# Two halves of a running sum on VectorE, and four later key-rounding steps on ScalarE

## The reference

```
q_hk = (hidden_q @ Wq.T).reshape(Bv, Sv, H, K)
q_big = jnp.einsum('bshk,hkq->bshq', q_hk, w_kc_q)          # then rope
kv_r = _apply_rope(kv_c, sin_k[None], cos_k[None])
q_r = jnp.einsum('bshq,hqr->bhsr', q_big, W_qr)
k_r = jnp.einsum('bld,hdr->bhlr', kv_r, W_kr)
scores = jnp.einsum('bhsr,bhlr->bhsl', q_r, k_r)
attn = jax.nn.softmax(scores, axis=-1)                       # over 1444 keys
ctx_c = jnp.einsum('bhsl,bld->bhsd', attn, kv_r)
```

## Time and profile before

| | us |
|---|---|
| median of 3 runs (3305.87 to 3306.35) | 3306.21 |
| time of the profiled execution | 3314.55 |
| its span | 3312.8 |
| mean granted TensorE clock | 0.929 of full |
| TensorE matmuls busy | 2855.9 (86%) |
| VectorE busy | 2276.1 (69%) |
| GpSimd busy | 1749.6 (53%) |
| ScalarE busy | 1658.2 (50%) |

### The profile page before, as it was taken

How to read it: one execution, slowest core, us unless ns; L and a number is a source line. 1 busy time by engine, 2 the same in 40 slices (tenths; PEclk the granted TensorE clock), 3 DMA queues, 4 the chain that set the end, 5 groups by cost and what they waited for, 6 DMA issues and landing times. The chain is left out here.

```text
span 3312.8 us, 62826 instructions
## 1 busy us (share of the span) xinstructions
PE 2855.9 (86%) x18352; PEld 1925.8 (58%) x18352; DVE 2276.1 (69%) x4050; ACT 1658.2 (50%) x3458; POOL 1749.6 (53%) x1268
## 2 busy tenths in 40 slices
PE   5999979999799899898998999899989989996335
PEld 4777769999655565565555555556556556553123
DVE  5778764444376676677677667767767667666887
ACT  1333322222147646647646655654764664663556
POOL 0000012322167757667666666766765766763566
PEclk9888879999899999999999999999999999998566
DMA  4000010000201100000100000010110100011100
GB/s 112 0 0 0 0 48 10 5 10 10 75 6 25 22 12 21 19 16 17 23 18 17 21 18 17 16 26 7 24 22 11 22 19 16 11 50 35 42 13 25
DMA packets 130259, 71.17 MB, mean 21 GB/s; under 512 B 83582, under 2 KB 124510, under 8 KB 129880
## 3 DMA queue, kind: packets, MB, share of 16 engines
q1 hardware_dynamic: 129944, 67.45, 8.2%
HBM read 56.95 MB, written 10.04 MB: 20 GB/s over the span
## 5 line engine op out<-in xcount | busy, mean ns | idle before, releaser
L1200 POOL TENSOR_TENSOR c_psum<-c_p 120x800 f32<-120x800 f32 (+1 forms) x384 | 758.4, 1980 | 454.3 <-ACT c_p L1514 199.8
L1514 ACT ACTIVATE c_p<-c_s_ps 120x400 f32<-120x400 f32 (+1 forms) x1536 | 650.9, 513 | 301.7 <-PE c_s_ps L1686 231.3
L1698 PE MATMUL c_o_ps<-c_p,c_val 120*64 120x400 f32 (+1 forms) x3072 | 614.8, 523 | 10.9 <-ACT c_onum L1479 10.9
L1279 DVE TENSOR_REDUCE c_mpart<-c_m_ps 128x1 f32<-128x484 f32 x416 | 271.4, 652 | 204.3 <-PE c_m_ps L1593 204.2
L1324 DVE TENSOR_TENSOR c_acc<-c_acc,c_psum 120x800 f32<-120x800 f32 x256 | 370.2, 1446 | 59.9 <-POOL c_psum L1200 57.9
L1593 PE MATMUL c_m_ps<-c_kmax,c_q 64*128 64x484 f32 x1080 | 308.4, 438 | 90.6 <-DVE c_mpart L1279 49.1
L1191 POOL TENSOR_TENSOR l_rr<-c_psum,l_rr 96x400 f32<-96x400 f32 x256 | 264.2, 1053 | 190.5 <-DVE l_rr L1346 190.4
L1698 PEld LDWEIGHTS c_o_ps<-c_p,c_val 120*64 120x64 f32 (+1 forms) x3072 | 191.5, 139 | 281.1 <-issue 163.5
L1682 PE MATMUL c_s_ps<-c_q,c_k 64*120 64x400 f32 (+1 forms) x1536 | 321.4, 370 | 1.7 <-ACT c_p L1514 1.7
L1285 DVE CUSTOM_DVE_ANT_0 c_xt<-c_m_ps,c_xt,c_mpart 128x484 fp32r<-128x484 f32 x360 | 259.8, 722 | 86.5 <-DVE c_mpart L1279 45.4
L1629 PE MATMUL c_s_ps<-c_xt,l_a 128*96 128x400 f32 x1536 | 310.4, 352 | 9.8 <-DVE l_rr L1346 8.0
(11 more groups left out here) (259 smaller groups left out, 5304.6 us busy)
## 6 DMA issues: line engine op xcount, KB each, us to landing
c_rdb<-l_denominators SPq DMA_DIRECT2D x128, 100.0 KB, 2.7
c_kv<-in_ctx SPq DMA_DIRECT2D x32, 360.0 KB
c_mrow<-c_mneg SPq DMA_DIRECT2D x288, 0.5 KB, 2.0
x_rows<-in_x SPq DMA_DIRECT2D x4, 800.0 KB
x_spill<-x_rows SPq DMA_DIRECT2D x8, 400.0 KB
l_xa<-x_spill SPq DMA_DIRECT2D x8, 400.0 KB
c_xr<-x_spill SPq DMA_DIRECT2D x32, 100.0 KB
x_spill<-c_xr SPq DMA_DIRECT2D x32, 100.0 KB
```

Of the source, the lines that this page charges most:

```text
L1200: g.tensor_tensor(psum[0:k, u % 2, :], p[0:k, 2 * u % 4, :], p[0:k, (2 * u + 1) % 4, :], ALU.add).then_inc(psum_ready, 1)
L1279: v.tensor_reduce(mpart[:, t:t + 1], m_ps[:, bank, 0:4 * KP], AX.X, ALU.max, negate=True).then_inc(mpart_ready, 1)
L1514: a.activation(p[0:k, w % 4, i * HALFQ:(i + 1) * HALFQ], s_ps[0:k, (2 * w + i) % 4, 0:HALFQ], ACT.Exp).then_inc(exp_ready, 1)
L1698: mm = pe.matmul(o_ps[i * DL:(i + 1) * DL, 0:HALFQ], val[0:k, j % 2, r, :], p[0:k, w % 4, i * HALFQ:(i + 1) * HALFQ], start=(r == 0), stop ...
```

## The change

`add_sums` gets an argument `half` and adds 400 columns (`HALFQ`) at a time. The first half of pair u-1's addition stands where the whole stood, behind the units of half 1 of pair u. The second half, which alone counts up `acc_ready`, stands behind the units of half 0 of pair u+1. The last ones of a group stand in the head. Of the rounding steps, 4, 5, 7 and 8 are done in the batch that uses the keys (in its tiles 1, 4, 3 and 5), and 1, 2, 3 stand at tiles 18, 20 and 21. `copy_keys` waits until all six steps of the batch before have read `kd`.

```diff
@@ -968,7 +968,7 @@
         AFTER_PROJECT = {next_in(2, units_at(j, 15).start): j for j in range(1, G - 1)}
 
         HEAD_STEPS = {10: (0, 1), 11: (2,), 12: (3,), 13: (4, 5), 15: (6, 7, 8)}
-        TILE_STEPS = {16: (0,), 17: (1,), 18: (2,), 19: (3,), 20: (4,), 21: (5,), 22: (6,), 23: (7,)}
+        TILE_STEPS, LATE_STEPS = {16: (0,), 18: (1,), 20: (2,), 21: (3,), 23: (6,)}, {1: (4,), 3: (7,), 4: (5,), 5: (8,)}
 
         def pairs():
             for u in range(NP):
@@ -1313,15 +1313,20 @@
                     v.wait_ge(xr_loaded[j], 16 * (n + 1))
                     v.scalar_tensor_tensor(xr[:, j, :], m_ps[0:S, 2, 0:D], m.tg[0:S, 1:2], xr[:, j, :], ALU.mult, ALU.add).then_inc(x_added, 1)
 
-                def add_sums(ch, q, n):
-                    k = keys_of(2 * q)
-                    v.wait_ge(psum_ready, PRIMED + n + 1)
+                def add_sums(ch, q, n, half):
+                    k, cols = keys_of(2 * q), slice(half * HALFQ, (half + 1) * HALFQ)
+                    if half == 0:
+                        v.wait_ge(psum_ready, PRIMED + n + 1)
+                        if q == 1:
+                            v.wait_ge(den_done, PRIMED + ch)
+                        if q > 1:
+                            v.wait_ge(acc_ready, PRIMED + ACC * ch + q - 1)
                     if q == 1:
-                        v.wait_ge(den_done, PRIMED + ch)
-                        v.tensor_tensor(acc[0:k, :], psum[0:k, 0, :], psum[0:k, 1, :], ALU.add).then_inc(acc_ready, 1)
+                        done = v.tensor_tensor(acc[0:k, cols], psum[0:k, 0, cols], psum[0:k, 1, cols], ALU.add)
                     if q > 1:
-                        v.wait_ge(acc_ready, PRIMED + ACC * ch + q - 1)
-                        v.tensor_tensor(acc[0:k, :], acc[0:k, :], psum[0:k, q % 2, :], ALU.add).then_inc(acc_ready, 1)
+                        done = v.tensor_tensor(acc[0:k, cols], acc[0:k, cols], psum[0:k, q % 2, cols], ALU.add)
+                    if q > 0 and half == 1:
+                        done.then_inc(acc_ready, 1)
 
                 def low_queries(gi, pair, src):
                     v.wait_ge(q1_ready, PRIMED + 4 * (gi * (H // 2) + pair + 1))
@@ -1335,7 +1340,9 @@
 
                 def head(gi, prev):
                     if prev:
-                        add_sums(gi * G * CH - 1, CP - 1, gi * NP - 1)
+                        add_sums(gi * G * CH - 1, CP - 2, gi * NP - 2, 1)
+                        for half in range(2):
+                            add_sums(gi * G * CH - 1, CP - 1, gi * NP - 1, half)
                     for i in range(H):
                         n = gi * H + i
                         v.wait_ge(wide_ready, PRIMED + n + 1)
@@ -1379,8 +1386,10 @@
                                 reduce_unit(it, n)
                             if u == 0 and half == 1:
                                 low_queries(it, H // 2 - 1, m_ps[:, 2, :])
+                            if half == 0 and u > 1:
+                                add_sums(ch if q > 1 else ch - 1, (q - 2) % CP, it * NP + u - 2, 1)
                             if half == 1 and u > 0:
-                                add_sums(ch if q > 0 else ch - 1, (q - 1) % CP, it * NP + u - 1)
+                                add_sums(ch if q > 0 else ch - 1, (q - 1) % CP, it * NP + u - 1, 0)
                         if (j, c) != (0, 0) and q == 2:
                             invert(ch - 1)
                         if (j, c) != (0, 0) and q == 5:
@@ -1399,7 +1408,9 @@
                     group(it, True)
                     head(it + 1, True)
                 group(NG - 1, False)
-                add_sums(B * CH - 1, CP - 1, NG * NP - 1)
+                add_sums(B * CH - 1, CP - 2, NG * NP - 2, 1)
+                for half in range(2):
+                    add_sums(B * CH - 1, CP - 1, NG * NP - 1, half)
                 done = [0]
 
                 def step(ins):
@@ -1444,6 +1455,7 @@
                                          src[i * DL:(i + 1) * DL, 0:T].rearrange("p (b s) -> p b s", b=G), ACT.Copy).then_inc(q1_ready, 1)
 
                 def copy_keys(b):
+                    a.wait_ge(k1_hi, PRIMED + b * 6)
                     for k in range(3):
                         a.wait_ge(kt_ready, PRIMED + b * 3 + k + 1)
                         a.activation(kd[:, k * 4 * KP:(k + 1) * 4 * KP], m_ps[0:DL, k, 0:4 * KP], ACT.Copy).then_inc(kf_ready, 1)
@@ -1529,8 +1541,8 @@
                                 for w in range(2 * u, 2 * u + 2):
                                     for n in TILE_STEPS.get(w % CT, ()) if j + 1 < G else ():
                                         round_steps(it * G + j + 1, j + 1, n)
-                                    if w % CT == 1 and j > 0:
-                                        round_steps(it * G + j, j, 8)
+                                    for n in LATE_STEPS.get(w % CT, ()) if j > 0 else ():
+                                        round_steps(it * G + j, j, n)
                     drain((it * G + G) * CH - 1)
 
                 head(0, False)
```

## The result

The changed kernel takes 3425.39 us (median of 4 runs, 3415.84 to 3429.66) against 3306.04 us before (4 runs): a ratio of 1.0357, 95% interval 1.0341 to 1.0372, or +119 us. The forecast was +36 us, with 3395 us as the upper end. The sign was right, the size was not. The profiled execution took 3424.66 us.

What follows compares the result with a forecast made beforehand. TensorE's order sets the pace (busy 86% of the span), so each new wait adds to the end. Denominators 21 + ring 16 + turns 20 - gain 24 + rounding 3 = +36 us, 3306 to 3342 us; range 3280 to 3395.

Steps and rivals of the forecast that it cites:

- Sign and chain: Slower, chance 0.67: second halves end later, so TensorE waits at the denominators and GpSimd, exponentials and rises come late.
- The ring: VectorE's addition, GpSimd's `add_pair`, exponentials two pairs on: GpSimd at q = 2 starts late, 2 us a group, 16 us.
- The denominators: Their matmuls at L1599 wait for a chunk's last addition, now ending later: 2.6 us a group, 21 us in all.
- The two halves follow each other: Pairs 7, 37, 43 have no low or mid in the first slot, so no new denominator wait: nothing taken.
- The ring at q = 0: GpSimd in pair 12 starts later and exponentials move by 1.1 us, but TensorE has other work: nothing taken.
- The gain: TensorE's waits for lows behind an addition shorten, as it ends 0.41 us sooner: 24 us saved, bounds 0 and 59.7.
- Taking turns: 320 more VectorE additions may meet GpSimd; 0.8 us for each of three batch ends, 2.5 us a group, 20 us.
- bare time: Two 400-column additions take 1.12 instead of 0.98 us a pair on VectorE: 46 us in all, with room on average.
- The rounding: Moved rounding steps end ScalarE's waits for `low_keys` without gain; step 7 is tight: 3 us of cost in all.
- Rival A: Bursts mattered: TensorE's waits for low and mid halve or better, 3276 us; needs L1599 waits under 0.1 us; chance 0.20.
- B: Nothing moves: buffers take up the later additions, gains and losses of 20 us cancel, 3306 us; chance 0.12.
- C: VectorE and GpSimd take turns at every half, TensorE waits 3 us more at 24 batch ends: 3394 us; chance 0.18.

Runs made afterwards that it cites:

- after: The changed kernel itself (additions cut in halves, second half later, rounding steps moved), against the kernel before: 3425.39 us, ratio 1.0357.
- q = 1 back: Changed kernel with both halves of the q = 1 addition put back in half 1 of pair u: 3359.01 us, +53 us against the kernel before.
- q = 2 both late: Changed kernel with both halves of the q = 2 addition in half 0 of the q = 4 pair: 3416.24 us, +108 us against the kernel before.
- the halves together: Kernel before with each addition cut in two halves, both in the old place, old rounding: 3363.66 us, ratio 1.0182.
- q = 1 and 5 back: Changed kernel with both halves of the q = 1 and q = 5 additions put back in half 1 of pair u: 3331.52 us, ratio 1.0091.
- the late middle additions: Kernel before with whole additions of q = 2, 3, 4 moved to half 0 of the pair after: 3281.27 us; with the rounding moved too 3291.32 us.

## Why the prediction missed

Point by point, by its own steps.

**Sign and chain: right.** The new wait at L1599 (now L1611), the late start of GpSimd at q = 2, the late exponentials of q = 4 and the rises behind them are all there, by the amounts worked out at pair 20. GpSimd's wait grew by 258 us (over 60 forecast), ScalarE's by 92.

**The ring: mis-sized, and the main failure.** The step was "That is 0.9 us of new wait ... I take 2 us a group, 16 us." It measured 66 to 67 us with the cut, and 86 us as a whole late addition without it. Two things failed in it. It took two places of a group at TensorE's wait for one unit, 0.9 us, where the means over the groups show the exponentials of q = 4 later by 0.9, 1.9, 1.7 and 1.4 us in four (pairs 4, 16, 22, 34), and earlier by 1.0 in one (pair 28). At 3>4 that is 4.6 us a group between after and q = 1 back, 37 us in all, against 16. And it took at nothing what VectorE's next additions meet when GpSimd is late, the 4.13 us above: at 4>5 and 5>0 the two kernels differ by another 3.8 us a group, 30 us. These three columns make 8.4 us a group, 67 us; over all six columns it is 7.3 us, 58 us. That the second part comes from VectorE's queue fits the run with q = 2 both late, where it was gone, but is not shown by itself.

**The denominators: the sum right, in part by luck.** 21 us forecast, 24 to 25 measured by the runs. In the second group TensorE waits 0.66 us in pair 13, 0.68 in 19 and 0.73 in 25 (0.5 forecast). In pair 31 it is 0.75, where over 1 us was forecast. The longest wait, 1.46 us, is in pair 43, which the forecast took at nothing:

```profile
1310.09 0.55 PE L1611 MATMUL c_m_ps<-c_acc,c_ones 121*32 121x200 f32 x8 [0.66 <-DVE c_acc L1327]
...
1394.59 0.55 PE L1611 MATMUL c_m_ps<-c_acc,c_ones 121*32 121x200 f32 x8 [0.75 <-DVE c_acc L1327]
...
1447.10 0.55 PE L1611 MATMUL c_m_ps<-c_acc,c_ones 121*32 121x200 f32 x8 [1.46 <-DVE c_acc L1327]
```

"The two halves follow each other" was the reason, and it is wrong there. VectorE does the row statistics of the next group (L49 to L55) between the first and the second half, from 1444.44 to 1446.57 us:

```profile
1444.44 1.40 DVE L49 BATCH_NORM_STATS2 c_stats<-l_xa 100x6 f32<-100x256 f32 x4
...
1446.48 0.57 DVE L1327 TENSOR_TENSOR c_acc<-c_acc,c_psum 120x400 f32<-120x400 f32 x1
```

The ring at q = 0, taken at nothing, is within these 24 us.

**The gain: it did not come.** "I take 24 us" from waits for lows that a shorter addition in front would shorten. The waits for lows grew, by 13 us in after and by 28 us with the halves together. A half lasts 0.91 us on average, 0.47 us less than the whole, but there are now two of them, in front of the lows of both slots, or 1.82 us in a row in the old place.

**Taking turns and bare time: direction right, too small.** VectorE spent 581 - 441 = 140 us more on the additions, between the 46 us of bare time and the 46 + 128 us of the bound. Priced at 20 us, with the gain 20 - 24 = -4; the cut alone measured +63. In after the late places of q = 2, 3, 4 give some of that back: with q = 1 and 5 back it is +28, where these two terms had -4.

**The keys' turn: not priced.** TensorE's wait there grew by 11 us.

**The rounding: within the noise.** 3 us forecast; +8 us alone (interval from -3 to +13), and no difference that the intervals tell on top of the late middle additions. ScalarE's waits for the low keys are gone and nothing is faster for it, as forecast.

The account by runs: 28 (cut, with the middle ones late) + 66 (q = 1) + 25 (q = 5) = 119 us. Of the 83 us that the forecast of 36 lacked, 50 lie in the ring and most of the others in the turns and the gain. Rival A fell by its own sign, the wait at L1599; B fell. C, the nearest in time, fell as a mechanism: it asked for a mean half over 1.1 us, and ScalarE's wait for `c_ct` rose only from 80.2 to 94.8 us. TensorE is also busy 30 us longer for the same 18352 matmuls; their ends are modelled, the clock of the second group's pairs is 0.96 against 0.97, and I leave open how much of it is real.

## What to carry to other kernels

In a ring of engines, price a late step at each place where it is late, by the whole delay of the stage that follows and not by the wait of the one instruction read; one fifth of the additions, moved behind one low and mid, cost 66 of the 119 us. Before an operation is cut to break a burst, ask whether its surplus comes from another engine's turn: then the cut buys a second turn. Ask of each position what stands right behind it on that engine: the same move cost 86 us at q = 1 and gave 27 us at q = 4, where the addition stood in front of what another engine waited for.

## What the runs showed of the hardware that I had not expected

- An 8-column VectorE addition of two SBUF tiles, 0.16 us in the median, took up to 1.89 us and 0.64 us on average when GpSimd worked beside it, and cost the kernel 46 us; a reduction of one tile, 0.176 us each, never lasted over 0.182 us.
- Two half additions in a row took 4.13 us for 1.12 us of work, and the second of them 3.30 us: it began at 1354.51 us, and ended after a GpSimd instruction that had begun before it and another that began at 1355.52. VectorE can lose the turn to GpSimd more than once.
- A wait made shorter (GpSimd at q = 0) made one kernel slower by 26 us at the same clock. In a second it came with 18 us, most of them in executions with a lower clock (0.920 to 0.923 against 0.926 to 0.930).
